# A vision transformer layer: the inverse norms of q and k from one GpSimd power instead of seven steps

## What is computed

```python
# x (32, 3, 96, 96), patches of 16 x 16: 32 x 36 = 1152 rows of 768 values, model width 192
p = img2patches(x, 16, 16)
h = layernorm(p) * ln1_g + ln1_b
h = einsum('bsd,dm->bsm', h, W) + b
h = layernorm(h) * ln2_g + ln2_b
# attention between the 32 images, for each patch position and each of 12 heads of 16
qkv = _layernorm(h) @ in_proj_weight.T + in_proj_bias
q, k, v = to_heads(...)
_normalize(t) = t / max(norm(t, axis=-1), 1e-12)
attn = einsum('nhld,nhmd->nhlm', _normalize(q), _normalize(k))
attn = softmax(attn * exp(min(logit_scale, log(100))))
o = einsum('nhlm,nhmd->nhld', attn, v) * head_scale
h = h + (o @ out_w.T + out_b)
# gated feed-forward with quantized rows and ternary weights, hidden width 512
h = h + bitlinear(silu(gate) * up, w_out, g_out),  up, gate = bitlinear(_layernorm(h), w_in, g_in)
```

## Time and profile before

| what | value |
|---|---|
| median of 3 runs | 126.71 us (126.38 to 126.77) |
| span of the profiled execution | 124.5 us |
| PE busy | 110.0 us (88%) |
| DVE busy | 104.1 us (84%) |
| ACT busy | 80.5 us (65%) |
| POOL busy | 73.4 us (59%) |
| chain that ended last | PE 51%, DVE 17%, POOL 11%, ACT 8% |

### The profile page before, as it was taken

One profiled execution on the slowest core, in us unless ns is written; L12 is line 12 of the kernel. 1 busy time (PEld: TensorE's weight loads), 2 busy tenths in 40 slices (PEclk: granted clock), 3 DMA queues, 4 the chain that ended last, 5 costly groups with the idle time before them and its releaser, 6 DMA issues.

```text
span 124.5 us, 4809 instructions
## 1 busy us (share of the span) xinstructions
PE 110.0 (88%) x1904; PEld 90.6 (73%) x1904; DVE 104.1 (84%) x338; ACT 80.5 (65%) x179; POOL 73.4 (59%) x172
## 2 busy tenths in 40 slices
...
DMA packets 24509, 7.68 MB, mean 62 GB/s; under 512 B 20579, under 2 KB 23909, under 8 KB 24486
## 3 DMA queue, kind: packets, MB, share of 16 engines
...
HBM read 6.48 MB, written 0.88 MB: 59 GB/s over the span
## 4 chain that ended last, share of the span: by engine, by line
PE 51%; DVE 17%; POOL 11%; ACT 8%; issue 6%; DMA 4%; DVEq 0%; POOLq 0%
PE bank L747 10%; PE bank L769 7%; PE bank L770 6%; PE bank L793 4%; DMA w_emb_sb<-in_L_tok_W_dram 4%; PE bank L781 3%; PE bank L829 3%; PE bank L655 3%; PE bank L727 2%; PE bank L669 2%; POOL yw L447 2%; PE bank L662 2%; ACT sq L576 2%; DVE ss L985 1%; PE bank L810 1%
## 5 line engine op out<-in xcount | busy, mean ns | idle before, releaser
L747 PE MATMUL bank<-w_emb_c,xT 128*128 128x192 f32 x108 | 19.3, 328 | 0.0
L747 PEld LDWEIGHTS bank<-w_emb_c,xT 128*128 128x128 f32 x108 | 17.4, 190 | 0.1
L655 PE MATMUL bank<-ones 128*128 128x128 f32 x84 | 13.1, 316 | 1.2 <-POOL ones L327 1.0
L379 POOL TENSOR_TENSOR rs<-mv,mhalf 128x1 f32<-128x1 f32 x9 | 5.1, 575 | 14.4 <-DVE mv L953 14.4
L655 PEld LDWEIGHTS bank<-ones 128*128 128x128 f32 x84 | 12.2, 227 | 1.8 <-POOL ones L327 1.0
L769 PE MATMUL bank<-w_qkv,xhT 97*128 97x384 f32 (+1 forms) x36 | 12.1, 417 | 1.6 <-DVE qkp L1022 1.5
L770 PE MATMUL bank<-w_qkv,xhT 96*128 96x384 f32 (+1 forms) x36 | 11.7, 405 | 0.0
L829 PE MATMUL bank<-wi_t,xqT 96*128 96x512 bf16 x36 | 9.3, 380 | 2.1 <-ACT xqT L600 1.9
L447 POOL TENSOR_TENSOR yw<-yy,gout_bc 128x512 f32<-128x512 f32 x8 | 10.2, 1273 | 0.6 <-DVE yy L1095 0.3
L769 PEld LDWEIGHTS bank<-w_qkv,xhT 97*128 97x128 f32 x36 | 6.1, 189 | 5.4 <-issue 1.9
L389 POOL TENSOR_TENSOR hg<-h0s,g_bc 128x192 f32<-128x192 f32 x9 | 5.2, 575 | 7.8 <-DVE h0s L960 7.7
...
## 6 DMA issues: line engine op xcount, KB each, us to landing
...
```

The source lines that it names most:

```text
L655: nc.tensor.matmul(spare_bank, ones[:, :], ones[:, :], start=True, stop=True)
L747: mm = nc.tensor.matmul(emb_bank, xT[:, t % 3, P * k:P * (k + 1)], w_emb_c[:, 3 * (k % 2) + k // 2, :], start=(k == 0), stop=(k == KF - 1))
```

## The change

The seven steps are replaced by one: POOL computes `rn` = `ssm` to the power -0.5, over all 24 columns of the tile, with the one-column constant `mhalf` broadcast. `qkn_` waits for it. The scaling of `ls_div` is dropped together with its constant, so `ssm_(0)` waits for the exponential and the memset themselves. `rn_` stands in POOL's list where `nw_` stood; all other calls keep their order. Lines of the changed kernel are lower than those of before by 8 to 40.

```diff
-RSQRT_BITS = 1596981248.0
-RSQRT_POLY = (-4.800725989352685, 9.406197882972911, -9.746409741798763, 6.813401626909552)
-NORM_SCALE = 7.142061302335728
...
-            def lsd_():
-                pool.wait_ge(p_lse, 1)
-                pool.wait_ge(c_div, 1)
-                nc.gpsimd.tensor_scalar(ls_div[:, :, :], ls_div[:, :, :], NORM_SCALE, None, ALU.mult).then_inc(p_lsd, 1)
...
-            def nw_(t):
-                pool.wait_ge(ng_ok, t + 1)
-                nc.gpsimd.tensor_tensor(out=rw[:, t, :], in0=ssm[:, t, :], in1=ry[:, t, :], op=ALU.mult).then_inc(nw_ok, 1)
-
-            def nv_(t):
-                pool.wait_ge(nw_ok, t + 1)
-                nc.gpsimd.tensor_tensor(out=rv[:, t, :], in0=rw[:, t, :], in1=ry[:, t, :], op=ALU.mult).then_inc(nv_ok, 1)
+            def rn_(t):
+                pool.wait_ge(ssm_ok, t + 1)
+                nc.gpsimd.tensor_tensor(out=rn[:, t, :], in0=ssm[:, t, :], in1=mhalf[:, :].to_broadcast([P, 2 * H]), op=ALU.pow).then_inc(rn_ok, 1)
...
             def ssm_(t):
                 if t == 0:
-                    dve.wait_ge(p_lsd, 1)
+                    dve.wait_ge(c_div, 1)
+                    dve.wait_ge(p_lse, 1)
                 dve.wait_ge(ss_ok, t + 1)
...
-            def ng_(t):
-                dve.wait_ge(ssm_ok, t + 1)
-                nc.vector.tensor_scalar(ry[:, t, :].bitcast(I32), ssm[:, t, :].bitcast(I32), -0.5, RSQRT_BITS, ALU.mult, ALU.add).then_inc(ng_ok, 1)
-
-            def np0_(t):
-                dve.wait_ge(nv_ok, t + 1)
-                nc.vector.scalar_tensor_tensor(out=rp[:, t, :], in0=rv[:, t, :], scalar=RSQRT_POLY[0], in1=rv[:, t, :],
-                                               op0=ALU.add, op1=ALU.mult).then_inc(np0_ok, 1)
...
-            def np3_(t):
-                dve.wait_ge(np2_ok, t + 1)
-                nc.vector.scalar_tensor_tensor(out=rn[:, t, :], in0=rp[:, t, :], scalar=RSQRT_POLY[3], in1=ry[:, t, :],
-                                               op0=ALU.add, op1=ALU.mult).then_inc(np3_ok, 1)
-
             def qkn_(t):
                 if t == 0:
                     dve.wait_ge(c_pad, 1)
-                dve.wait_ge(np3_ok, t + 1)
+                dve.wait_ge(rn_ok, t + 1)
```

More of the change, by code:

```diff
@@ L11 @@
 I16 = mybir.dt.int16
-I32 = mybir.dt.int32
 P = 128
@@ L127, in vit_layer @@
         ssm = sb("ssm", [P, T, 2 * H])
-        ry = sb("ry", [P, T, 2 * H])
-        rw = sb("rw", [P, T, 2 * H])
-        rv = sb("rv", [P, T, 2 * H])
-        rp = sb("rp", [P, T, 2 * H])
         rn = sb("rn", [P, T, 2 * H])
```

69 lines of the change are left out of this document (31 added, 38 removed).

## The result

The changed kernel takes 158.2 us (median of four executions; 156.5 to 160.1) beside 126.6 us for the kernel before on the same chip: 1.245 times as long, interval 1.240 to 1.250. The direction was right, the size was not: 133.5 us was forecast, and the range ended at 155. The profiled execution took 156.52 us with a span of 154.7 us (before: 124.5), and TensorE's granted clock was 0.907 of full speed on the mean in it. That clock differs from one execution to the next in this kernel and its relatives, so all comparisons from here on leave out executions more than 1.5% above the fastest of the same kernel (the kernel after then has 157.9 us), and of the profiles of `c18`, `dead`, `late`, `nmfirst` and `nmhold`, which come from such executions, only the order of events is used.

What follows compares the result with a forecast made beforehand. PE was taken to bound 45 to 65 us, and POOL's nearly unbroken work the end. Upstream 1.36 plus POOL's 5.4 gave 6.8 us, so 126.71 + 6.8 = 133.5 us; range 125.0 to 155 us.

Steps and rivals of the forecast that it cites:

- there once: Low end for the power on POOL: its 0.35 us over a one-column product comes once, 24 columns take 0.60 us.
- each column has it anew: High end for the power on POOL: every column pays the 0.35 us again, 24 columns take 8.6 us.
- d: Duration of one 24-column power on POOL, taken as 2.5 us.
- 4d - 4.6: POOL's added lateness from tile 5 to the end, four powers less removed products and pauses: 5.4 us at 2.5 us each.
- Tiles 0 and 2: The power delays `qkp`, at tile 2 also through `rs` and `h_all`, and PE waits: +0.56 and +0.8 us.
- The turning point at 1.15 us: Power duration that decides on POOL: below it the kernel gets faster, above it POOL is late.
- Tiles 1, 3 and 4 ... I cost them at nothing: Over 2 us of other DVE work, or slack at PE, covers the power there; gone at a 3.5 us power.
- the bare sum: Upstream loss at tiles 0 and 2 plus POOL's later lateness, 1.36 + 5.4 = 6.8 us, on 126.71 us.
- The power stops DVE: Rival: the power holds up `h_all` or `xc` at tiles 1, 3 and 6, 2 us more, 135.5 us; chance 0.12.
- The cases from 5.3 us of d up: Slower still, powers of 5.3 us and longer towards column after column (8.6 us), up to 187 us; chance 0.15.
- the cases (3.5 to 5.3, 140 to 156 us): Power of 3.5 to 5.3 us on POOL, kernel at 140 to 156 us; chance 0.15.

Runs made afterwards that it cites:

- c18: The changed kernel with the power on 18 of the 24 columns, the rest constant: 144.93 us, ratio 1.141 to the kernel before.
- dead: The kernel before with its seven steps kept, plus an unread 24-column power behind each `rv` in POOL's list: 159.1 us, ratio 1.253.
- late: The changed kernel with 24 columns in the powers of tiles 5 to 8 only, one column at tiles 0 to 4: 139.6 us (single execution).
- nmfirst: The changed kernel with POOL's `nm` of tiles 6, 7 and 8 ahead of the powers of tiles 4, 5 and 6: 153.8 us (single execution).
- nmhold: The changed kernel with `nm` of tiles 6 to 8 and `rs` of tile 5 ahead of powers, plus 65 unread matmuls on PE: 151.3 us, ratio 1.193.
- c12: The changed kernel with the power on 12 of the 24 columns, the rest constant: 133.07 us, ratio 1.048 to the kernel before.
- hold: The changed kernel with 65 unread matmuls of 128 columns ahead of seven of PE's waits: 154.9 us, ratio 1.221 to the kernel before.
- early: The changed kernel with 24 columns in the powers of tiles 0 to 4 only, one column at tiles 5 to 8: 141.0 us.
- c1: The changed kernel with the power on one of the 24 columns, the rest constant: 124.67 us, ratio 0.982 to the kernel before.
- c6: The changed kernel with the power on 6 of the 24 columns, the rest constant: 126.65 us, ratio 0.999 to the kernel before.
- t13: The changed kernel with 24 columns in the powers of tiles 1 and 3 only, one column elsewhere: 128.3 us, ratio 1.015 to the kernel before.
- t4: The changed kernel with 24 columns in the power of tile 4 only, one column elsewhere: 130.0 us, ratio 1.025 to the kernel before.
- t4nm: The changed kernel with 24 columns at tile 4 only, and POOL's `nm` of tile 6 moved ahead of that power: 125.98 us, ratio 0.996.
- experiment 8: The kernel before with its polynomial of degree 4 shortened to degree 3, then to degree 2: 125.98 us (ratio 0.996) and 124.57 us (ratio 0.983).

## Why the prediction was right or wrong

**The duration of the power: wrong, and the first cause.** 2.5 us was taken between 0.60 and 8.6, 4.17 is measured. The step that failed is the split of the 0.35 us which the first column of a power has over a product's: the prediction weighed "there once" against "each column has it anew" and took a value near the root of the two. About two fifths of it come again with each column (0.16 of 0.38). The reason it gave for the low side held only as far as "not as cheap as 2 ns". The estimate worked out from the Trainium skill (GPSIMD Engine Reference, § 7 Performance pitfalls for Q7 kernels), which took the columns for the page's independent chains and came to 2.6 us for the whole, fell too: 0.156 us a column from 1 to 24 and 0.159 on to 192, where that estimate had 0.09.

**Where the time went, by stretches.** The table has the time from `ssm` of one tile to `ssm` of the next, and from `ssm` of tile 5 to the end of the span, in us. Its second row adds to the kernel before what the prediction's steps give for d = 4.17: 2.2 us at tile 0, 2.5 at tile 2, nothing at tiles 1, 3 and 4, and 4d - 4.6 = 12.1 behind.

| kernel | tile 0 | 1 | 2 | 3 | 4 | sum | tile 5 to the end |
|---|---|---|---|---|---|---|---|
| before | 6.50 | 8.79 | 9.63 | 7.18 | 8.15 | 40.2 | 55.8 |
| the prediction's steps at 4.17 | 8.7 | 8.8 | 12.1 | 7.2 | 8.2 | 44.9 | 67.9 |
| after | 10.48 | 10.98 | 13.50 | 9.12 | 13.76 | 57.8 | 68.6 |
| `c12` | 6.90 | 9.09 | 10.88 | 7.22 | 9.15 | 43.2 | 59.8 |
| `hold` | 8.79 | 10.97 | 12.70 | 9.72 | 12.49 | 54.7 | 69.9 |
| `early` | 9.42 | 10.98 | 13.64 | 10.20 | 12.49 | 56.7 | 54.4 |
| `c1` | 6.02 | 8.82 | 9.73 | 7.42 | 8.16 | 40.2 | 54.4 |

**Tiles 0 and 2: right in the path, too small in size.** `qkp` of tile 0 and PE's wait stand where the steps put them, and at tile 2 `h_all` waits 3.8 us for POOL's `rs`, as written. But the two cost 4.0 and 3.9 us, not 2.2 and 2.5. What the prediction left out at tile 0 is the clock: where it is kept up (`hold`) tile 0 costs 2.3 us, nearly the figure of the steps. At tile 2 `hold` has 3.1.

**Tiles 5 to 8 by POOL's load, 4d - 4.6: right.** Behind `ssm` of tile 5 the kernel after takes 12.8 us more than before, for 12.1, and `late` has +14.9 against `c1` for +14.4. The turning point at 1.15 us fits `c6`.

**"Tiles 1, 3 and 4 ... I cost them at nothing": wrong, and the second cause.** This is the step of the path that failed. They cost 2.2, 1.9 and 5.6 us in the kernel after, 9.7 together; alone, tiles 1 and 3 cost 3.6 (`t13`) and tile 4 5.3 us (`t4`). Two things are in it. At tiles 1 and 3 there was cover, but only as long as the way from `ssm` to `qkp` had been, 2.37 and 2.48 us; it is 4.57 and 4.55 now, and what is over is paid. The prediction said that this cover is gone at d = 3.5, and its 140 us there is 0.5 us above the bare sum (139.5), its 156 at 5.3 us 5.7 above (150.3); between them about 2.5 us at 4.17, a quarter of what was due. At tile 4 it asked who waits for the power, and not who waits for what stands behind the power: there the release runs over `nm`, `xh`, `xqT`, PE, `th`, `yg` and `kT`, and `t4nm` takes 4.0 of 5.3 us away with one scalar moved. The prediction had done just that for tile 2 (`rs`, then `h_all`), and for tile 5 it named the scalars behind the power, as POOL's lateness only.

**The account at 4.17 us.** The sum with the right d gives 4.7 + 12.1 = 16.8 us and so 143.5 (146 with what its own figures for larger d add), and 157.9 are measured. So of the 24.4 us above the forecast of 133.5, 10 go to the duration by the sum's own terms, and 14.4 to the sum. In the traces, the span grew by 30.2 us. Of the 13.6 that the sum lacks in the table, 9.7 are at tiles 1, 3 and 4, 3.2 at tiles 0 and 2, and 0.7 behind. The clock is in both of the first two: `hold` takes 3.2 us away ahead of tile 5, 1.7 of them at tile 0, and gives 1.3 back behind, where its own matmuls stand too. How much of the whole is clock stays open.

**The test that the prediction set itself.** "The sum with the right d should still give the time": it gives 143.5 to 146 and not 158. "Wrong in the mechanism if POOL has pauses of over 1 us behind tile 5 and the kernel is slower all the same": behind tile 5 it has one, of 1.15 us, and around tile 4 it had two, of 2.74 and 3.02 us. POOL's load sets the end, as forecast, but 17.6 us, more than half of the loss, are made ahead of tile 5's `ssm`, by others' waits, while POOL itself is not full.

**The power stops DVE: didn't happen.** DVE and POOL in the timeline of the kernel after, at tile 7:

```profile
108.49 4.19 POOL L388 TENSOR_TENSOR rn<-ssm,mhalf 128x24 f32<-128x24 f32 x1
...
109.75 0.23 DVE L1009 RECIPROCAL rsum<-bank 128x12 f32<-128x12 f32 x1
109.89 0.35 DVE L1032 SCALAR_TENSOR_TENSOR xc<-h_all,mv,gin_s 128x192 f32<-128x192 f32 x1
...
110.16 0.35 DVE L1013 TENSOR_TENSOR on<-bank,rsum 128x192 f32<-128x192 f32 x1
```

The power of tile 7 ran from 108.49 for 4.2 us, and `xc`, a DVE instruction with two inputs in SBUF, took 0.35 us in the middle of it, no more than its mean of 0.40 over nine tiles. The rule of the Trainium skill (SBUF — State Buffer, § SBUF: two separate sides), a lock for the whole instruction, is not borne out for this one. It does fit POOL's wide product `yw` of 512 columns: the earlier trace rows, and experiment 8, where `rn` is held up to the end of `yw` when it begins behind its start and takes 0.17 us when it begins ahead. At tiles 1 and 3, where the prediction placed this rival, DVE began `h_all` and `xc` 0.16 us ahead of the power, as it had argued.

**The range.** The cases from 5.3 us of d up had been given 15 in 100 and the range cut at 155; d itself lay inside the cases (3.5 to 5.3, 140 to 156 us). The time was missed because the sum's own error at large d wasn't in the bounds.
